# A corner's middle products in another PSUM bank, side work in other slots, and a low-rank update whose batches overlap

## The reference, cut to what matters

```python
def step(Sm, inp):
    q_, k_, v_, g_, b_ = inp
    Sm = Sm * jnp.exp(g_)[..., None, None]
    kv = jnp.einsum('bhk,bhkv->bhv', k_, Sm)
    delta = (v_ - kv) * b_[..., None]
    Sm = Sm + jnp.einsum('bhk,bhv->bhkv', k_, delta)
    o = jnp.einsum('bhk,bhkv->bhv', q_, Sm)
    return (Sm, o)
```

```python
x_diff = x[:, None, :, :] - select_mean_diff[None, :, None, :]
x_diff = x_diff / jnp.linalg.norm(x_diff, axis=3, keepdims=True)
cont = jnp.einsum('nds,bntd->bnts', select_weight, x_diff) ** 2
score = cont.sum(axis=-1)
gate = jax.nn.sigmoid(imp_slope[None, :, None] * (score - imp_center[None, :, None]))
sel_scale = gate.max(axis=1)[..., None]
sel_idx = gate.argmax(axis=1)
...
mod_x = jnp.einsum('btdh,btd->bth', upd, x - debias)
degen_up = jnp.einsum('btdh,bth->btd', dgn, mod_x)
return (1.0 - sel_scale) * x + sel_scale * ETA * (bias + degen_up)
```

## Time and profile before

| | |
|---|---|
| time, median of 3 runs | 5528.94 us (5526.64 to 5529.01) |
| time of the profiled execution | 5525.55 us |
| its span | 5523.8 us |
| PE busy | 4907.9 us (89%) |
| PEld, DVE, ACT, POOL busy | 62%, 57%, 49%, 31% |
| TensorE clock granted, mean | 0.934 of full speed |

### The profile page before, as it was taken

One profiled execution on the slowest core, in us unless ns is written; L12 is line 12 of the kernel. 1 busy time (PEld: TensorE's weight loads), 2 busy tenths in 40 slices (PEclk: granted clock), 3 DMA queues, 4 the chain that ended last, 5 costly groups with the idle time before them and its releaser, 6 DMA issues. The chain is left out here.

```text
span 5523.8 us, 136894 instructions
## 1 busy us (share of the span) xinstructions
PE 4907.9 (89%) x56862; PEld 3436.8 (62%) x56862; DVE 3134.3 (57%) x5368; ACT 2727.1 (49%) x6857; POOL 1711.4 (31%) x1899
## 2 busy tenths in 40 slices
PE   5799999999999999999987997899987894699979
PEld 4577777777777777777775555555554453355545
DVE  4666666666666666666665664555535554443231
ACT  2565665666656666666653443454432334245521
POOL 0445544555545455455440001011103120012210
PEclk7899999999999999999998998999998896788779
DMA  2000000000000000000001001000000000000000
GB/s 98 15 24 21 20 21 20 21 25 22 20 17 25 22 21 21 20 20 22 25 16 46 1 1 71 1 0 0 0 22 19 12 1 14 24 1 1 1 23 16
DMA packets 51138, 106.45 MB, mean 19 GB/s; under 512 B 12960, under 2 KB 20032, under 8 KB 49376
## 3 DMA queue, kind: packets, MB, share of 16 engines
q1 hardware_dynamic: 50528, 97.84, 5.7%
HBM read 90.20 MB, written 5.52 MB: 17 GB/s over the span
## 5 line engine op out<-in xcount | busy, mean ns | idle before, releaser
L972 ACT ACTIVATE dh_lv<-bank_pair 128x768 f32<-128x768 f32 (+1 forms) x640 | 491.7, 768 | 311.5 <-PE bank_pair L759 246.6
L1274 POOL TENSOR_TENSOR dh_qi<-dh_lv,dh_ids 128x256 f32<-128x256 f32 x512 | 404.3, 794 | 390.8 <-ACT dh_lv L972 390.8
L1088 DVE SCALAR_TENSOR_TENSOR dh_kq<-bank,dh_conv_kq,dh_kq 128x511 f32<-128x511 f32 (+2 forms) x408 | 305.3, 748 | 157.4 <-ACT dh_kq L927 147.8
L759 PEld LDWEIGHTS bank_pair<-dh_lv 64*64 64x64 f32 x14336 | 256.1, 134 | 201.3 <-issue 178.1
L1272 POOL TENSOR_TENSOR dh_qi<-dh_lv,dh_ids 128x512 f32<-128x512 f32 x128 | 170.2, 1329 | 587.5 <-ACT dh_lv L972 587.5
L321 POOL TENSOR_TENSOR ln_rstd<-ln_var_eps,nhalf 128x4 f32<-128x4 f32 x32 | 34.3, 1072 | 1008.3 <-DVE ln_var_eps L304 1008.3
L759 PE MATMUL bank_pair<-dh_lv 64*64 64x64 f32 x14336 | 325.8, 225 | 16.3 <-ACT dh_lv L972 16.3
L1088 DVE SCALAR_TENSOR_TENSOR dh_v<-bank,dh_conv_v,dh_v 128x511 f32<-128x511 f32 (+2 forms) x384 | 285.3, 746 | 77.9 <-ACT dh_v L927 68.8
L667 PE MATMUL bank<-hT,dh_w_kq 128*128 128x512 f32 x544 | 262.7, 606 | 15.8 <-DVE dh_kq L1088 8.4
L851 PE MATMUL bank<-dh_wo_gated,dh_ww 128*128 128x256 f32 x1040 | 260.4, 394 | 4.3 <-DVE dh_qkm L1131 4.3
L679 PE MATMUL bank<-dh_w_vz,hT 128*128 128x256 f32 x1024 | 252.0, 389 | 13.3 <-ACT dh_ww L948 13.3
(11 more groups left out here) (473 smaller groups left out, 12244.0 us busy)
## 6 DMA issues: line engine op xcount, KB each, us to landing
dh_rates<-delta_rates SPq DMA_DIRECT2D x130, 256.0 KB, 3.3
dh_w_vz<-in_L_wvz SPq DMA_DIRECT2D x17, 512.0 KB, 3.3
mod_w<-in_L_wmod SPq DMA_DIRECT2D x4, 1536.0 KB, 7.2
dh_w_kq<-in_L_wkq SPq DMA_DIRECT2D x18, 256.0 KB, 2.5
dh_wo<-in_L_wo SPq DMA_DIRECT2D x16, 256.0 KB, 4.1
moe_w<-in_L_w13T SPq DMA_DIRECT2D x1, 3200.0 KB, 15.9
later_gates<-mod_gate SPq DMA_DIRECT2D x3, 1024.0 KB, 4.0
gate<-later_gates SPq DMA_DIRECT2D x6, 512.0 KB, 3.8
```

The lines of the kernel that those rows point to most:

```text
L759: last = pe.matmul(lvl[g][halves[g ^ o], sl, kind, :], lhs, rhs, start=True, stop=True)
L972: act.activation(out, src, ACT.Copy).then_inc(hs[j]["a_lv"], 1)
L1088: dve.scalar_tensor_tensor(y, pj_bank(q, n)[:, 0:S - i], taps(n)[:, TAPS - 1 - i:TAPS - i], y, ALU.mult, ALU.add).then_inc(s["v_cs" if i < ...
L1274: pool.tensor_tensor(out[:, :, 0, :], src[:, :, 0, :], mask_bc(ids[:, :], NB), ALU.add).then_inc(h["p_qi"], 1)
```

## The change

In the delta stage `cross` writes to bank 3 (`PJ_A`) in place of bank 2, and waits for the convolutions that read bank 3. `turn_c` of head 0 no longer waits for `cross_copy`. At the head of a stage `v_turn` of head 0 stands before `corner`, and `qs` of head 0 before `z_prod` of head 1, with a wait of its own. Slot 8 moves behind `level` 4 of head 0 and `qk_prod`. In stages with a=3 the last of the four transposes of q, with its squares and sum, moves from slot 5 to slot 7.

```diff
-    merged = [... for i in (*LEVEL, TURN)]
+    merged = [... for i in (*LEVEL, PJ_A)]
     def turn_c(pe, t, j):
         after(pe, hs[j]["v_u"], t)
         if j == 0:
-            after(pe, s["a_g"], t)
+            after(pe, hs[1]["a_ct"], t)
+            if t % NC == 2:
+                pe.wait_ge(s["v_cv"], count(t // NC, V_ITEMS + 4))
     def cross(pe, t):
-        if t % NC == 1: pe.wait_ge(s["v_cv"], count(t // NC, V_ITEMS + 4))
+        if t % NC < 3:
+            pe.wait_ge(s["v_cv"], count(t // NC, (V_ITEMS - 1, V_ITEMS + 3, ITEMS)[t % NC]))
     def qs(pe, t, j):
-        if j:
+        if j == 0:
+            pe.wait_ge(hs[1]["a_vs"], t + 1)
+        else:
             pe.wait_ge(hs[0]["v_qs"], carried(t))
-        if a == 3 and 2 <= f < 6: turn_kq(pe, q, 2 + f)
+        if a == 3 and 2 <= f < 5: turn_kq(pe, q, 2 + f)
+        if a == 3 and f == 7: turn_kq(pe, q, f)
     # the same for squares on ScalarE and norms on VectorE
     def tensor_stage(pe, t):
         turn_c(pe, t, 0)
+        v_turn(pe, t, 0)
         if t: corner(pe, t - 1)
-        v_turn(pe, t, 0)
...
         first_level(pe, t, 0)
+        if old: qs(pe, t, 0)
         z_prod(pe, t, 1)
-        if old: qs(pe, t, 0)
...
         side_tensor(pe, q, a, 7)
-        side_tensor(pe, q, a, 8)
         level(pe, t, 4, 0)
         qk_prod(pe, t)
+        side_tensor(pe, q, a, 8)
         level(pe, t, 4, 1)
     # scalar_stage
         side_scalar(act, q, a, 7)
+        level_copy(act, t, 4, 0)
         side_scalar(act, q, a, 8)
-        level_copy(act, t, 4, 0)
```

```diff
+    # TensorE
+                for b in range(2):
+                    turn(b)
+                    project(b)
+                for b in range(NB):
+                    if b + 2 < NB: turn(b + 2)
+                    turn_picked(b)
+                    if b + 2 < NB: project(b + 2)
+                    lower(b)
+    # ScalarE
+                tokens(0)
+                score_squares(0)
+                tokens(1)
+                for b in range(NB + 1):
+                    if b < NB: distances(b, 0)
+                    if b: gate(b - 1)
+                    if b < NB: distances(b, 1)
+                    if b: picked(b - 1)
+                    if 0 < b < NB - 1: tokens(b + 1)
+                    if b < NB:
+                        distances(b, 2)
+                        last_squares(b)
+                    if b < NB - 1: score_squares(b + 1)
+                def last_squares(b):
+                    act.wait_ge(s["pf"], 2 * b + 2)
+                    after(act, s["rd"], b)
+                    act.activation(square[:, :, :], diff[:, NC - 1, :, :], ACT.Square).then_inc(s["nn"], 1)
+    # VectorE
+                def apart(b, t):
+                    dve.wait_ge(s["tok"], 2 * b + t // 2 + 1)
+                    after(dve, s["nn"], NC * (b - 1) + t + 1 if b else 0)
+                    dve.tensor_tensor(diff[:, t, :, :], mask_bc(htok[:, b % 3, t, :], N), mb[:, :, :], ALU.subtract)\
+                        .then_inc(s["df"], 1)
+                def score(b):
+                    c, n = sc[:, b % 2, :, :], nd[:, b % 2, :, :, :]
+                    dve.wait_ge(s["nn"], NC * (b + 1))
+                    dve.tensor_reduce(n[:, 0, NC - 1, :], square[:, :, :], AX_X, ALU.add).then_inc(s["rd"], 1)
...
+                apart(0, 0)
+                apart(0, 2)
+                apart(1, 0)
+                for b in range(NB):
+                    score(b)
+                    if b + 1 < NB: apart(b + 1, 2)
+                    pick(b)
+                    if b + 2 < NB: apart(b + 2, 0)
+                    add(b)
+    # GpSimd
+                for b in range(NB):
+                    for t in (1, 3):
+                        pool.wait_ge(s["tok"], 2 * b + t // 2 + 1)
+                        after(pool, s["nn"], NC * (b - 1) + t + 1 if b else 0)
+                        pool.tensor_tensor(diff[:, t, :, :], mask_bc(htok[:, b % 3, t, :], N), mb[:, :, :], ALU.subtract)\
+                            .then_inc(s["pf"], 1)
-        with nc.Fori(0, NB) as b:
-            with Phase(nc, "lora_run") as p2:
```

More of the change, by code:

```diff
@@ L1026, in side_scalar @@
         if a == 3 and f < 2: silu_z(act, q, 6 + f)
-        if a == 3 and 2 <= f < 6: squares(act, q, 2 + f)
+        if a == 3 and 2 <= f < 5: squares(act, q, 2 + f)
+        if a == 3 and f == 7: squares(act, q, f)
     def side_silu(act, q, a, f):
@@ L1215, in side_vector @@
         if a == 2 and f < 8 and f % 2: norms(dve, q, f // 2)
-        if a == 3 and 2 <= f < 6: norms(dve, q, 2 + f)
+        if a == 3 and 2 <= f < 5: norms(dve, q, 2 + f)
+        if a == 3 and f == 7: norms(dve, q, f)
     def vector_stage(dve, t):
@@ new lines, in pick @@
+                def pick(b):
+                    i = b % 2
+                    dve.wait_ge(s["sig"], b + 1)
+                    for t in range(NC):
+                        dve.max(m8[:, i, t, :], gt[:, i, t, :]).then_inc(s["top"], 1)
+                    dve.wait_ge(s["top"], NC * (b + 1))
+                    dve.tensor_copy(key[:, i, :, 0:1], m8[:, i, :, 0:1]).then_inc(s["keys"], 1)
+                    dve.wait_ge(s["keys"], b + 1)
+                    for t in range(NC):
+                        dve.match_replace(mr[:, i, t, :], key[:, i, t, :], gt[:, i, t, :], -2.0).then_inc(s["mark"], 1)
+                    dve.wait_ge(s["mark"], NC * (b + 1))
+                    after(dve, s["bt"], b - 1)
+                    dve.tensor_scalar(bb[:, i, :, R:R + N], mr[:, i, :, :], -2.0, None, ALU.is_equal).then_inc(s["pick"], 1)
+                    dve.wait_ge(s["pick"], 2 * b + 1)
+                    for t in range(NC):
+                        last = dve.tensor_tensor(grouped(bb[:, i, t, 0:R]), grouped(pr_bank(b)[:, t, R:P]),
+                                                 row_bc(bb[:, i, t, R:R + N], LN_S), ALU.mult)
+                    last.then_inc(s["pick"], 1)
@@ new lines, in add @@
+                def add(b):
+                    dve.wait_ge(s["out"], b + 1)
+                    for i in range(2):
+                        dve.scalar_tensor_tensor(y[:, 2 * i:2 * i + 2, :], htok[:, b % 3, 2 * i:2 * i + 2, :], -1.0,
+                                                 k.bank[5 + i][:, :].rearrange("p (t d) -> p t d", t=2), ALU.mult, ALU.add)\
+                            .then_inc(s["yo"], 1)
+                    dve.wait_ge(s["yo"], 2 * (b + 1))
+                    dve.tensor_tensor(y[:, :, :], y[:, :, :], row_bc(m8[:, b % 2, :, 0], D), ALU.mult).then_inc(s["ym"], 1)
+                    dve.wait_ge(s["ym"], b + 1)
+                    dve.tensor_tensor(y[:, :, :], y[:, :, :], htok[:, b % 3, :, :], ALU.add).then_inc(s["ya"], 1)
+                    dve.wait_ge(s["ya"], b + 1)
+                    add_gated(dve, k, 1, b, [y[:, 2 * i:2 * i + 2, :].rearrange("p t d -> p (t d)") for i in range(2)],
+                              tmp, s["tmp"], s["fin"], 2 * b)
```

210 lines of the change are left out of this document (98 added, 112 removed).

## The result

| | median us | executions | profiled execution: us / span |
|---|---|---|---|
| before | 5528.98 | 5526.64 to 5531.53 | 5525.55 / 5523.8 |
| after | 5466.74 | 5461.53 to 5472.61 | 5463.59 / 5461.9 |

The ratio is 0.9888, with a 95% interval from 0.9871 to 0.9905: 62 us faster, where 78 were forecast (5451). The time lies in the range of 5412 to 5488.

A forecast was written before the change was run, and what follows sets the result against it. TensorE's work and idle time were taken to bound the delta stage, a chain of waits the low-rank update. 39 + 39 = 78 us off the profiled 5525.55 gives 5447.6, so 5451 at the median; 8 in 10 range 5412 to 5488.

The forecast's parts named there:

- the chain through `project`: Low-rank update: VectorE's chain through `project` sets the period; the prediction called itself wrong if it does not.
- Stage head: Delta stage, `turn_c` and `v_turn` ahead of `corner`: 0.37 us won at 44 boundaries, 0.07 at 16, 17.4 us in all.
- `qs` ahead of `z_prod`: Delta stage, head 1: about 1 us of TensorE's work put ahead of the 0.47 wait removes it, 21 us won.
- Slot 8: Delta stage, a=2, behind `qk_prod`: waits of 0.5, 0.3 and 0.2 replace one of 0.83, a loss of 2 us.
- Slot 5 to 7: Delta stage, a=3: transposes fill half the wait before `level` 4, but the later mask limits `w_out`; +3 us.
- Update: Low-rank update: 153.9 us becomes 114.8 (fill 31.5, periods 26.5, 26.5 and 18.1, end 12.2), a gain of 39 us.
- Hold-up: Low-rank update: two-input instructions of GpSimd and VectorE wait for each other, 3.7 us a batch, twice, and 2.6 in the fill.
- Table loads: ScalarE in the low-rank update: one load of 1.28 us in all, where there were 8.
- the third: Rival, chance 0.12: update held up more, by GpSimd's 5.9 a subtraction or two table loads a batch; 130 us, time 5466.
- The second: Rival, chance 0.14: the delta stage's new order gives nothing, as its waits only move; time 5490.
- the fourth: Rival, chance 0.03: slower, as `v_turn` waits for `collect` and everything of the stage waits behind it; time 5543.
- The first: Rival, chance 0.10: everything hidden, GpSimd and VectorE don't meet, delta waits go whole; time 5383.

The follow-up runs named there:

- e3: Kernel after with `corner` put ahead of `v_turn` again at the stage head; 5431.9 us, ratio 0.9821 to the kernel before.
- e6: Kernel after with the update's projection of batch b + 2 moved behind `lower` of batch b, GpSimd's part kept; 5461.2 us.
- e5: Kernel after with all sixteen subtractions of the low-rank update on VectorE and none on GpSimd; 5447.7 us.
- e1: Kernel before with the delta stage's edits alone, the low-rank update left as it was; 5499.4 us, ratio 0.9949 to the kernel before.
- e4: Kernel after with three orders undone: `qs` behind `z_prod`, slot 8 ahead of `level` 4, last turn of q in slot 5; 5493.6 us.
- e7: Kernel after with `corner` ahead of `v_turn`, all update subtractions on VectorE, and the projection behind `lower`; 5414.2 us, ratio 0.9785 to the kernel before.
- e11: e7 unchanged, run and profiled again; 5422.2 us, ratio 0.9803 to the kernel before.

## Why the prediction was right, and where it was off

The direction, the two parts and most of the waits that go and come were right. Two steps were not: the new order at the stage head gave a third of its term, and the update's period is not set by the chain through `project`, which the prediction itself had named as a sign of being wrong. The forecast of 78 us became 62 by these terms:

- **Stage head: 17.4 forecast, 5.4 measured** (16 x (0.18 + 0.17 + 0.17 - 0.18)). This is the step that failed. "`corner` and `v_turn` take 1.11" was read where `v_turn` came last; with `corner` last they take 1.19, and the product behind pays 0.1 more. After a=0 the expected +0.07 so became -0.18. `collect`'s end, on which I spent the argument, was right to 0.01 in both kinds of boundary. e3 shows the step that was missing altogether: the copy of `cross` is ready before `collect` ends, so the wait of 0.58 was free to be filled by `corner`. The Trainium skill ("TensorEngine Tiling (Array Packing)", "Key Properties") says that a change of the tiling mode drains TensorE. The trace is in line with it, though it shows only the cost: each first group of products of 128 rows behind products of 64 rows takes some 0.06 to 0.1 more (0.66 and 0.60 for four turns, 2.05 and 1.95 for `ks`).
- **`qs` ahead of `z_prod`: 21 forecast, 24.5 measured** (16 x 1.53). The wait of 0.47 went whole, and 0.07 more with it.
- **Slot 8: -2 forecast, +1.9 measured.** The three waits came as told, 0.43, 0.26 and 0.13 for 0.5, 0.3 and 0.2; each was a little over-estimated, and that turned the sign.

```profile
1646.65 0.46 PE L761 MATMUL bank_pair<-dh_lv 64*64 64x64 f32 x16 [0.43 <-ACT dh_lv L978]
1647.61 1.16 PE L639 MATMUL bank<-dh_kq 128*128 128x128 f32 x8 [0.26 <-DVE dh_kkm L1133]
```

- **Slot 5 to 7: +3 forecast, +2 measured**, by another way than told. `w_out` of a=3 has no wait (it starts at 1691.40; the mask ended at 1690.52 + 0.69), so the mask behind the norms is not the limit, and that sign failed. What the trace shows: in slot 7 the turn is hidden whole, for `level` 4 starts 1.44 behind `level` 3's last products in both kernels, and the stage is 0.43 shorter where the turn had stood. But `level` 4's products of GpSimd's sum now start 0.54 behind its first ones and not 0.25, because they wait for that sum; with it 0.3 goes back, and 0.13 is left.

```profile
1687.65 0.32 PEld L761 LDWEIGHTS bank_pair<-dh_lv,dh_qi 64*64 64x64 f32 x16 [0.22 <-POOL dh_qi L1282]
```

The four delta terms add to 33.9, taken 16 times each; the stage won 32.6. Between the first and the last `cross` there are only 15 stages with a=0, and three of them, at the ends of rounds, won less than 0.71.

- **Update: 39 forecast, 36.8 measured.** Periods 26.1, 26.1, 18.0 and the end 12.0, for 26.5, 26.5, 18.1 and 12.2; the fill 35.0 for 31.5. The 2.6 of hold-up that I had put behind the squares came as 1.6, in a small multiplication (below), but the folded weights were forgotten: they read two tensors of SBUF, GpSimd had begun, and the projection, and so the first squares, waited 5.0 us for them. GpSimd's subtraction takes 4.51 (4.7 forecast), the long square 1.90 (1.9), the sum 2.28 (2.3). The period agrees to 0.4, and its two terms nearly: 8.0 and 8.6 from the picks to the product for 8.7, 4.0 and 3.5 of hold-up for 3.7. But one can't be won without the other. In e6 the first is 2.3 shorter and the hold-up grows to 6.1 (3.10 + 5.42 for 2 x 1.23). So beside GpSimd it is the end of its second subtraction that sets the period, and not the chain through `project`.

```profile
4600.97 1.76 DVE L3270 TENSOR_TENSOR lora_score<-lora_score,lora_norm 128x32 f32<-128x32 f32 x1
4602.77 0.19 DVE L3272 TENSOR_TENSOR lora_score<-lora_score,lora_slope_center 128x32 f32<-128x32 f32 x1
```

- **Hold-up.** Forecast 3.7 for the multiplication, measured 4.03 and 3.45 (5.26 and 4.68 less 1.23), and e5 removes it. The rule of the Trainium skill that the prediction cited ("SBUF — State Buffer", "Who interferes with whom") agrees with the runs in its exception too: an instruction of VectorE with one SBUF input is not held up (L3298 and L3263 above).
- **Table loads.** One in the update, 1.28 us, ahead of the first sigmoid, where before had eight: as forecast. The prediction had added that two loads in a block of such instructions would mean that no set has them all. The kernel before had two in each pass, one ahead of the copies and one ahead of the sigmoid, though one set does serve them all here; why it loaded twice, no run shows.

```profile
L3230 ACT ACT_TABLE_LOAD x1 | 1.3, 1283 | 0.0
```

- **The setup**, 8.5 us of the profiled execution, was in no term. With it taken out the two profiled executions differ by 70.5. The medians hold some of it too: the eight executions of the kernel after in two groups lie between 5457.4 and 5472.6, those of before between 5525.7 and 5538.0; the fastest of each are 68 apart.

Of the rivals, the third named a time of 5466, which is the measured one, but by a mechanism that did not come: the update took 117 us, not 130, since GpSimd's subtraction took 4.51 in the median and 6.65 only twice in eight. The second (the delta order gives nothing) falls with e1 and e4. Of the fourth, the wait for `collect` came, but at 0.18 us in three of four boundaries and 0.56 in the others it was far from making the kernel slower. The first did not come; e3 shows only that the wait at the head could go whole.

## What to carry to other kernels

When a wait is taken away by another order, write down for each instruction that moves when its inputs are ready, and fill the new wait with the one that is ready first; and count a further 0.06 to 0.1 us, as here, wherever products of another tile shape now follow each other. Before GpSimd is given half of VectorE's work, look whether the two read SBUF with two inputs at the same time: here its help made the update 14 us longer than VectorE alone did, and the whole 10. And align the traces by stage before explaining a difference of totals, through to the end: 8 us were in a setup that nobody had touched, and another 4 to 7 of e5 to e7 in the code behind the update, which nobody had touched either.

## What the runs showed of the hardware

- A VectorE `tensor_tensor` of 128 x 128 values that began 0.02 us behind the start of a GpSimd subtraction took 4.62 us (L3315, least 0.23): a short instruction paid the whole of the other's 4.49.
- ScalarE's long activations were not held up by GpSimd: the square of 2048 took 1.90 to 1.91 us, both in the kernel after, beside GpSimd's subtractions, and in e5, without them.
- The granted clock of TensorE, busy without a pause from 21 us, was 1.00 until 70 us in some executions and 0.66 from 40 us in others of the same program; over the profiles the setup ended up to 11.5 us apart (81.3 against 69.8).
- An edit changed the time of untouched code behind it, and TensorE's granted clock there (0.50 for 0.65 in its first 20 us): with the update of e5, e6 and e7 the untouched stretch behind it took 775.8, 779.6 and 779.5 us, with that of the kernel after 772.2 and with that of before 773.4; e7's value came back in e11 (779.4).
